# A three-part transformer kernel on one core: two gate products of the first mixture move from VectorE to GpSimd, and a copy moves one step later

## The chip, the cores and the metric

The kernel runs on one core of a Trainium2 chip. The metric is the device time of one execution in microseconds (us). The kernel before takes 2415.65 us, the median of 3 runs (2415.49 to 2415.98). In profiles the engines are PE (TensorE's matmuls), PEld (its weight loads), DVE (VectorE), ACT (ScalarE), POOL (GpSimd) and SP (SyncE, which issues all transfers).

## What is computed

4096 tokens of 256 features go through half a mixture of experts, an attention block with its own small feed-forward, and half the same mixture again, all in float32.

```python
def _L0_ffn_ref(x, gate_W, W1, b1, W2, b2, Ws1, bs1, Ws2, bs2, route_scale):
    B, S, D, E, H, K = (4, 512, 256, 8, 128, 2)
    scores = jax.nn.sigmoid(x @ gate_W) * route_scale
    topk_scores, topk_idx = jax.lax.top_k(scores, K)
    topk_w = topk_scores / topk_scores.sum(-1, keepdims=True)
    gate_full = jnp.einsum('bsk,bske->bse', topk_w, one_hot(topk_idx, E))
    h = jax.nn.gelu(jnp.einsum('bsd,edh->bseh', x, W1) + b1, approximate=False)
    y = jnp.einsum('bseh,ehd->bsed', h, W2) + b2
    shared = jax.nn.gelu(x @ Ws1 + bs1, approximate=False) @ Ws2 + bs2
    return jnp.einsum('bse,bsed->bsd', gate_full, y) + shared
...
x = x + 0.5 * _L0_ffn_ref(_layernorm(x), ...)
x = x + _L0_attn_ref(_layernorm(x), ...)
x = x + 0.5 * _L0_ffn_ref(_layernorm(x), ...)
```

## The kernel before

Four phases follow one another: the first mixture (names with `f_`, `tail` set), attention (`a_`), a small feed-forward (`m_`) and the second mixture (`g_`, the same function `ffn_phase` with `tail` not set). Instructions are written out by hand for each engine, in the order in which the engine runs them, and the engines meet at counted semaphores. An engine that waits holds up all that stands behind it on that engine.

A mixture handles the 4096 tokens in 8 blocks of 512. Blocks 0 and 1 are written out, blocks 2 to 5 are a loop over pairs, 6 and 7 are written out again. A block has nine steps: step 0 is the shared expert, steps 1 to 8 are the experts. For step e

- TensorE computes the hidden layer `hid` (`first_layer`, L938, 6 matmuls of 512 columns), and, two steps behind, the second layer of step e - 2 into `acc` (`second_layer`, L980, 12 matmuls of 256 columns). The second layer of step 7 runs in step 0 of the next block;
- ScalarE applies the gelu (L515), then, one step behind in `f_`, rounds the gated result to its high part (`hi`, L507);
- VectorE multiplies the gelu's result by the gate (`gating`, L737), and makes the low part (`lo`, L742), which in `f_` belongs to the step before and in `g_` from block 1 on mostly to the same step. The second layer waits for `lo`.

From block 2 on the gate of a token, laid out along the partitions, comes from SBUF (`gB`, filled by a transfer); in blocks 0 and 1 (`on_pe`) TensorE makes it in PSUM (`gbc`). So from block 2 on `gating` has two SBUF operands. `lo` has two SBUF operands always.

Between the steps VectorE does work for other blocks: the choice of the top two experts for block i + 1 (`choices` at step 3, `gates` at step 4, L701 to L720: a chain of small operations on 32 columns), the layer norm statistics and normalisation of block i + 2 (`x_stats` at step 6, `x_norm` at step 7, L652, which needs a power from GpSimd, L592), the copy of the stacked gates (`gate_stack`, L727, out of PSUM, at the step that `STEADY["stack"]` names), and in `f_` the statistics of the rows for attention (`z_stats` at step 2, `zz_stats` at step 5). GpSimd has only the powers and small products around them: L606 for the sigmoid, L589 to L602 for the norms. ScalarE's `z_norm` (step 4) and `zn_norm` (step 7), four operations each (L446), stand between its gelus. At step 8 of blocks 1 to 7 of `f_` TensorE transposes `zn` (L905 into `aux`). In block 1 that bank holds the stacked gates, so the transposes wait there for the copy of them:

```python
                if e == 8 and tail and not first:
                    if on_pe(i):
                        pe.wait_ge(s["gst"], i + 2)
                        pe.wait_ge(s["gf"], i)
```

In the other blocks TensorE waits for the copy only in step 0 of the next block, before it overwrites the bank. The code follows.

Of the kernel before, what the change touches and what calls it, by code (L numbers as in the profile page):

```python
# [23 lines left out]
ALU = mybir.AluOpType  # L24
# [8 lines left out]
E, HID = 8, 128  # L33
NE = E + 1
# [11 lines left out]
def stand_alone(eng, turns):  # L46


    eng.sem_inc(turns, 1)
# [75 lines left out]
def ffn_phase(nc, turns, tag, src, dst, w, tail):  # L125
# [17 lines left out]
    if tail:  # L143
# [21 lines left out]
        gated = m.sb("gated", [P, 3, BT], room=rooms.second)  # L165
# [9 lines left out]
        act_out = m.sb("act_out", [P, 3, BT], room=rooms.wide)  # L175
# [3 lines left out]
        gB = m.sb("gB", [P, E, BT], room=rooms.rows)  # L179
        gf = m.sb("gf", [P, BT], room=Rooms().loads)  # L180
# [14 lines left out]
    else:  # L195
# [9 lines left out]
        gB = m.sb("gB", [P, E, BT], room=rooms.wide)  # L205
        gf = m.sb("gf", [P, BT], room=rooms.wide)
# [7 lines left out]
        act_out = m.sb("act_out", [P, 3, BT], room=rooms.first)  # L214
        gated = m.sb("gated", [P, 3, BT], room=rooms.first)
# [30 lines left out]
    s = {n: m.sem(n) for n in names.split()}  # L246
# [7 lines left out]
    def shared(e):  # L254
        return e == 0

    def weights_of(e):
# [7 lines left out]
    PRODUCTS_AT = {2: 0, 3: 1, 5: 2}  # L265
    SUMS_AT = {3: 0, 4: 1, 6: 2}

    STEADY = dict(up_x=0, logits=1, neg=2, choices=3, gates=4, up_gates=6, gf=6, stack=6)
    FIRST = dict(stats=1, norm=2, up_x=3, logits=4, neg=5, choices=7, gates=7, up_gates=8, stack=8) if tail else \
        dict(stats=0, norm=1, up_x=2, logits=3, neg=4, choices=6, gates=7, up_gates=8, stack=8)  # L270

    def now(what, e, first):

        return (FIRST if first else STEADY).get(what) == e

    def has(i, ahead=0):

        return not isinstance(i, int) or 0 <= i + ahead < NB

    def on_pe(i):  # L280

        return isinstance(i, int) and i < 2

    def up_bank(i):

        return aux if on_pe(i) else gbc

    def over_blocks(eng, body):
        body(0, 0, True, False)
        body(1, 1, False, False)  # L290
        with eng.Fori(0, (NB - 4) // 2) as it:
            body(it * 2 + 2, 0, False, False)
            body(it * 2 + 3, 1, False, False)
        body(NB - 2, 0, False, False)
        body(NB - 1, 1, False, True)
# [274 lines left out]
    def on_gpsimd(pool):  # L570

        def first_fills():
            pool.memset(b2_in[:], 0.0)
            pool.memset(mhalf[:], -0.5)
            pool.memset(ebase[:], E_NUM)

        def pad():

            pool.memset(gpad[:], 0.0).then_inc(s["padded"], 1)
            pool.wait_ge(s["padded"], 1)  # L580
            pool.memset(gpad[:, :, 2 * E:LOW + E + 1:LOW - E], 1.0).then_inc(s["padded"], 1)
            pool.wait_ge(s["padded"], 2)

        def rstds(stats, ready, rstd, veps, powed, n, minus_mean=None):

            pool.wait_ge(ready, n)
            stand_alone(pool, turns)
            if minus_mean is not None:
                pool.tensor_scalar(minus_mean[:], stats[:, :, 0], -1.0, 0.0, ALU.mult, ALU.add)  # L589
            pool.tensor_scalar(rstd[:], stats[:, :, 1], EPS, None, ALU.add).then_inc(veps, 1)  # L590
            pool.wait_ge(veps, n)
            pool.tensor_tensor(rstd[:], rstd[:], mhalf[:], ALU.pow).then_inc(powed, 1)  # L592

        def x_rstd(i):
            rstds(mv, s["stats"], rs, s["veps"], s["rstd"], i + 1)

        def z_rstds(i, which):

            n = i * 2 + which + 1
            rstds(zmv, s["z_stats"], zrs, s["z_veps"], s["z_rs"], n, zshift)  # L600
            pool.wait_ge(s["z_rs"], n)
            pool.tensor_tensor(zshift[:], zshift[:], zrs[:], ALU.mult).then_inc(s["z_rstd"], 1)  # L602

        def expneg(i):
            pool.wait_ge(s["neg"], i + 1)
            pool.tensor_tensor(nl[:].rearrange("p t e -> p (t e)"), ebase[:],  # L606
                               nl[:].rearrange("p t e -> p (t e)"), ALU.pow).then_inc(s["expneg"], 1)

        def body(i, par, first, last):
            if first:  # L610
                x_rstd(1)
            if not last:
                expneg(i + 1)
            if tail and not first:
                z_rstds(i - 1, 0)
                z_rstds(i - 1, 1)
            if has(i, 2):
                x_rstd(i + 2)
        if tail:
            first_fills()  # L620
            pad()
            x_rstd(0)
        else:
            whole.mlp["gpsimd"](pool, dict(pad=pad, x_rstd=lambda: x_rstd(0), expneg=lambda: expneg(0)))
        over_blocks(pool, body)
        return dict(z_rstds=lambda which: z_rstds(NB - 1, which))

    def on_vector(dve):
# [100 lines left out]
        def gating(i, e):  # L729
            dve.wait_ge(s["gelu"], i * NE + e + 1)  # L730
            if on_pe(i):
                dve.wait_ge(s["gbc"], i * E + e)
                gate = gbc[:, (e - 1) % 2]
            else:
                dve.wait_ge(s["gates_in%d" % ((e - 1) // (E // 2))], (i - 1) * 16)
                gate = gB[:, e - 1]
            dve.tensor_tensor(gated[:, e % 3], gate, act_out[:, e % 3], ALU.mult).then_inc(s["gated"], 1)  # L737

# [88 lines left out]
        def body(i, par, first, last):  # L827
            for e in range(NE):
                if not last and now("neg", e, first):
                    neg_logits(i + 1, up_bank(i))  # L830
                if not shared(e):
                    gating(i, e)
                if e == 1 and not first:

                    result(i - 1)
                behind = not (tail or first) and e not in (0, 3, NE - 1)
                if tail or first:
                    if e > 0 and not (tail and first and e == 1):
                        lo(i, e - 1)
                    elif e == 0 and not first:  # L840
                        lo(i - 1, NE - 1)
                else:
                    if e == 0 and isinstance(i, int) and i == 1:
                        lo(0, NE - 1)
                    if not behind:
                        lo(i, e)
                if e == 0 and first:
                    gate_stack(0, 0, aux)
                if tail and first and e == 0:
                    qkv_bias(gbc[:, 1], 1, FIRST_BIAS)  # L850
                    w2_low(slice((NE - 1) * D, NE * D))
                if tail and first and e == 1:
                    w2_low(slice(0, (NE - 1) * D))
                if not last:
                    if now("stats", e, first):
                        x_stats(i + 1, 1 - par)
                    if now("norm", e, first):
                        x_norm(i + 1, 1 - par, False)
                    if now("up_x", e, first):
                        xt_lo(i + 1, 1 - par, up_bank(i))  # L860
                if tail and not first:
                    if e == 2:
                        z_stats(i - 1)
                    if e == 5:
                        zz_stats(i - 1)
                if not last:
                    if now("choices", e, first):
                        choices(i + 1)
                    if now("gates", e, first):
                        gates(i + 1)  # L870
                if has(i, 2):
                    if e == 6:
                        x_stats(i + 2, par)
                    if e == 7:
                        x_norm(i + 2, par, False)
                if not last and now("stack", e, first):
                    gate_stack(i + 1, 1 - par, up_bank(i))
                if tail and not first and e == 8:
                    for c in range(DC):
                        zt_lo(i - 1, c, aux[:, c])  # L880
                if tail and first and e == 2:
                    dve.wait_ge(s["qkv_in"], 64)
                    dve.tensor_scalar(ln[:, 0, :, 0], ln[:, 0, :, 0], QS, None, ALU.mult).then_inc(s["qs"], 1)
                    dve.wait_ge(s["qs"], 1)
                if tail and (first or last):
                    for k, c in QKV_AT.get((first, e), ()):
                        qkv_lo(k, c)
                if tail and last and e in SUMS_AT:
                    bias_sum(SUMS_AT[e])
                if behind:  # L890
                    lo(i, e)
# [1393 lines left out]
```

## Time and profile before

| | |
|---|---|
| median of 3 runs | 2415.65 us |
| the profiled execution | 2414.72 us, its span 2412.9 us |
| TensorE's granted clock | 0.999 of full speed |
| busy share of the span | PE 98%, PEld 86%, DVE 77%, ACT 70%, POOL 63% |
| first mixture | from 0 to about 276 us |
| second mixture | from about 2145 us to the end |
| period of a block, `f_` | about 31.4 us (block 4 to block 5) |
| period of a block, `g_` | about 29.5 us |

The span is from the first to the last instruction. A row of the timeline names the start in us, the duration, the engine, the line, the operation with its output and inputs, and how many like it follow one another. Idle time ahead of it, with what ended it, stands in brackets. In one engine's rows a start may lie up to 0.1 us before the end of the row above, since operations overlap a little.

### The profile page before, as it was taken

Reading aid. Unit: us, or ns where it says so; the run is one execution under the profiler, and the core shown is the slowest. Engines: PE = TensorE matmul, PEld = TensorE weight load, DVE = VectorE, ACT = ScalarE, POOL = GpSimd, SP = SyncE. Lnnn points to the kernel's source line nnn. Section 1 sums busy time; section 2 is a strip of 40 time slices with the busy share of each in tenths; the row PEclk is TensorE's granted clock in tenths of the full one; section 3 lists DMA queues with packets and bytes.
Section 4 is the critical chain, followed back from the end, with each engine's and each line's share of the span. In section 5 each row is a group of like instructions: output and inputs, shape, how many; then the busy total and the mean of one; then the engine's idle time right before and its main releaser. Section 6 shows DMA issues by size and latency. Waiting matters only on the chain.

```text
span 2412.9 us, 46345 instructions
## 1 busy us (share of the span) xinstructions
PE 2374.6 (98%) x14512; PEld 2068.2 (86%) x14512; DVE 1867.4 (77%) x3615; ACT 1684.6 (70%) x2932; POOL 1521.8 (63%) x1536
## 2 busy tenths in 40 slices
PE   8999999999999999999999999999999999999999
PEld 7888878888888888888888888888888889998898
DVE  7887687888878788887878878788887875466775
ACT  4555677877878787787878778787787865443444
POOL 1333368787777877778787777878777765542220
PEclk9999999999999999999999999999999999999999
DMA  4744631222212232221223312122221345431332
GB/s 181 264 165 156 211 114 45 96 80 78 96 44 87 61 96 75 64 96 44 87 62 97 102 36 96 44 87 84 82 96 44 110 165 166 137 116 58 130 125 95
DMA packets 131970, 245.67 MB, mean 102 GB/s; under 512 B 7290, under 2 KB 90132, under 8 KB 120052
## 3 DMA queue, kind: packets, MB, share of 16 engines
q1 hardware_dynamic: 131828, 244.15, 31.0%
q8 instruction: 44, 0.72, 0.1%
q14 instruction: 98, 0.80, 0.1%
HBM read 140.12 MB, written 53.67 MB: 80 GB/s over the span
## 4 chain that ended last, share of the span: by engine, by line
PE 83%; DVE 7%; issue 4%; POOL 3%; ACT 2%; DMA 2%; SPq 0%; DVEq 0%; POOLq 0%; ACTq 0%
PE a_ov L1727 20%; PE a_sc L1691 19%; PE a_tr L1703 19%; PE a_pj L1638 7%; PE a_pj L1645 4%; PE g_acc L980 3%; PE g_hid L938 3%; PE f_acc L980 2%; PE f_hid L938 2%; PE m_proj L2141 1%; POOL m_zin L1987 1%; PE m_hid L2210 1%; DMA f_xin<-in_x 1%; DVE f_hp L742 1%; DVE f_gated L737 1%
## 5 line engine op out<-in xcount | busy, mean ns | idle before, releaser
L1594 DVE TENSOR_REDUCE a_nmax<-a_sc 128x1 f32<-128x1024 f32 x512 | 626.8, 1224 | 252.1 <-PE a_sc L1691 248.3
L1437 ACT ACTIVATE a_pT<-a_tr 128x512 fp32r<-128x512 f32 x1024 | 559.6, 596 | 317.2 <-PE a_tr L1703 312.3
L1521 POOL TENSOR_SCALAR a_pr<-a_pr,a_rden 128x1024 f32<-128x1024 f32 x512 | 576.5, 1127 | 282.3 <-DVE a_rden L1599 212.1
L1605 DVE TENSOR_TENSOR a_pT<-a_tr,a_pT 128x512 fp32r<-128x512 f32 x1024 | 650.4, 677 | 17.1 <-ACT a_pT L1437 17.1
L1727 PE MATMUL a_ov<-a_pT,a_v_s 128*128 128x512 f32 x2032 | 594.1, 414 | 1.2 <-DVE f_zT L784 0.8
L1443 ACT ACTIVATE a_pr<-a_sc,a_nmax 128x1024 f32<-128x1024 f32 x512 | 573.7, 1121 | 20.2 <-DVE a_nmax L1594 17.9
L1691 PE MATMUL a_sc<-a_k_s,a_q_s 128*128 128x512 f32 x2048 | 556.6, 393 | 0.6 <-DMA a_k_s<-a_k_s 0.6
L1703 PEld LDWEIGHTS a_tr<-f_ident,a_pr 128*128 128x128 f32 x4096 | 476.0, 140 | 79.8 <-DVE a_pT L1605 7.3
L1703 PE MATMUL a_tr<-f_ident,a_pr 128*128 128x128 f32 x4096 | 537.1, 273 | 1.8 <-DVE a_pT L1605 1.7
L1691 PEld LDWEIGHTS a_sc<-a_k_s,a_q_s 128*128 128x128 f32 x2048 | 376.6, 188 | 76.7 <-DMA a_k_s<-a_k_s 0.8
L1727 PEld LDWEIGHTS a_ov<-a_pT,a_v_s 128*128 128x128 f32 x2032 | 343.8, 189 | 47.5 <-issue 4.8
L1638 PE MATMUL a_pj<-a_z_s,a_wqk_s 128*128 128x512 f32 x756 | 213.9, 392 | 1.5 <-ACT a_staged L1398 1.1
L1638 PEld LDWEIGHTS a_pj<-a_z_s,a_wqk_s 128*128 128x128 f32 x756 | 141.6, 188 | 33.7 <-ACT a_staged L1398 1.4
L980 PEld LDWEIGHTS f_acc<-f_w2p,f_hp 128*128 128x128 f32 x864 | 110.8, 190 | 19.5 <-DVE f_hp L742 14.6
L980 PE MATMUL f_acc<-f_w2p,f_hp 128*128 128x256 f32 x864 | 117.2, 285 | 7.4 <-DVE f_hp L742 7.1
L980 PEld LDWEIGHTS g_acc<-g_w2p,g_hp 128*128 128x128 f32 x864 | 111.9, 191 | 11.3 <-DVE g_hp L742 6.8
L980 PE MATMUL g_acc<-g_w2p,g_hp 128*128 128x256 f32 x864 | 115.7, 284 | 3.4 <-DVE g_hp L742 3.2
L1645 PEld LDWEIGHTS a_pj<-a_wv_s,a_z_s 128*128 128x128 f32 x756 | 105.8, 188 | 12.1 <-issue 0.7
L938 PE MATMUL f_hid<-f_xT,f_w1p 128*128 128x512 f32 x432 | 113.7, 398 | 0.0
L938 PE MATMUL g_hid<-g_xT,g_w1p 128*128 128x512 f32 x432 | 113.0, 397 | 0.0
L515 ACT ACTIVATE f_act_out<-f_hid,f_b 128x512 f32<-128x512 f32 x72 | 49.1, 684 | 91.0 <-PE f_hid L938 91.0
L1645 PE MATMUL a_pj<-a_wv_s,a_z_s 128*128 128x256 f32 x756 | 109.0, 280 | 0.3 <-ACT a_q_s L1405 0.3
(265 smaller groups left out, 3182.0 us busy)
## 6 DMA issues: line engine op xcount, KB each, us to landing
a_z_s<-zT SPq DMA_DIRECT2D x32, 1024.0 KB, 7.8
a_k_s<-a_k_s SPq DMA_DIRECT2D x62, 512.0 KB, 5.6
a_wqk_s<-w_split SPq DMA_DIRECT2D x64, 256.0 KB, 3.1
a_v_s<-a_v_b SPq DMA_DIRECT2D x16, 1024.0 KB, 4.6
att<-a_ao SPq DMA_DIRECT2D x32, 512.0 KB, 2.9
m_in<-att SPq DMA_DIRECT2D x16, 1024.0 KB, 5.9
f_gB<-f_gate_rows SPq DMA_DIRECT2D x12, 1024.0 KB, 4.9
g_gB<-g_gate_rows SPq DMA_DIRECT2D x12, 1024.0 KB, 4.7
```

What stands on the lines that cost most here:

```text
L938: o = pe.matmul(hid[:, (par + e) % 2], w1p[:, a, (c * NE + x) * HID:(c * NE + x + 1) * HID], xT[:, par, c, b], start=(n == 0), stop=(n == 5))
L980: o = pe.matmul(acc[:, t], hp[:, e % 3, a, t * P:(t + 1) * P], w2p[:, b, x * D:(x + 1) * D], start=False, stop=(e == NE - 1 and (a, b) == ...
L1437: act.activation(pT[:, (u // 4) % 2, 0, 4 * part:4 * part + 4, (u % 4) * P:(u % 4 + 1) * P], tr[:, part].rearrange("p (t q) -> p t q", t=4 ...
L1443: act.activation(pr[:, k % NP], sc[:, k % 2], ACT.Exp, bias=nmax[:, k % NP:k % NP + 1], accum_out=den[:, k % NP:k % NP + 1]).then_inc(s["e ...
L1521: pool.tensor_scalar(pr[:, k % NP], pr[:, k % NP], rden[:, k % NP:k % NP + 1], 1.0, ALU.mult, ALU.mult).then_inc(s["normed"], 1)
L1594: dve.tensor_reduce(nmax[:, k % NP:k % NP + 1], sc[:, k % 2], AX.X, ALU.max, negate=True).then_inc(s["negmax"], 1)
L1605: dve.tensor_tensor(to[:, 1], tr[:, part].rearrange("p (t q) -> p t q", t=4), to[:, 0].bitcast(F32), ALU.subtract).then_inc(s["tr_lo"], 1)
L1638: o = pe.matmul(bank[:], wqk_s[:, "QK".index(kind), h, a], z_s[:, h * 2 + b, part], start=(h == 0 and i == 0), stop=(h == 1 and i == 2), s ...
L1645: o = pe.matmul(bank[:, h * 2 * P:(h + 1) * 2 * P], z_s[:, c * 2 + a, part // 2, col:col + P], wv_s[:, c, b], start=(i == 0), stop=(i == 5))
L1691: o = pe.matmul(sc[:, k % 2, kb * BT:(kb + 1) * BT], q_s[:, slot, head, tile * P:(tile + 1) * P], k_s[:, slot, head, a, kb * BT:(kb + 1) * ...
L1703: o = pe.transpose(tr[:, part, j * P:(j + 1) * P], pr[:, (k - LAG) % NP, (4 * part + j) * P:(4 * part + j + 1) * P], ident[:])
L1727: o = pe.matmul(values_bank(v, last)[:], v_s[:, vslot, kt, 2 * vhead:2 * vhead + 2] .rearrange("p k f -> p (k f)"), pT[:, blk % 2, a, kt], ...
```

## The change

The products of the gates of experts 4 and 5 are issued by GpSimd in the first mixture's blocks 2 to 7, between its two groups of small operations for the norms. They write the same buffers and count on the same semaphore `gated`. VectorE leaves out these two, and its product for expert 6 waits until both are counted. In the steady blocks (1 to 6) of both mixtures the copy of the stacked gates moves from step 6 to step 7, where it stands after `x_norm`.

```diff
-    STEADY = dict(up_x=0, logits=1, neg=2, choices=3, gates=4, up_gates=6, gf=6, stack=6)
+    STEADY = dict(up_x=0, logits=1, neg=2, choices=3, gates=4, up_gates=6, gf=6, stack=7)
...
+    POOL_GATES = (4, 5)
...
+        def gating(i, e):
+
+            pool.wait_ge(s["gelu"], i * NE + e + 1)
+            pool.wait_ge(s["gated"], i * E + e - 1)
+            pool.wait_ge(s["gates_in%d" % ((e - 1) // (E // 2))], (i - 1) * 16)
+            stand_alone(pool, turns)
+            pool.tensor_tensor(gated[:, e % 3], gB[:, e - 1], act_out[:, e % 3], ALU.mult).then_inc(s["gated"], 1)
+
...
             if tail and not first:
                 z_rstds(i - 1, 0)
+                if not on_pe(i):
+                    for e in POOL_GATES:
+                        gating(i, e)
                 z_rstds(i - 1, 1)
...
                 dve.wait_ge(s["gates_in%d" % ((e - 1) // (E // 2))], (i - 1) * 16)
+                if tail and e == POOL_GATES[-1] + 1:
+
+                    dve.wait_ge(s["gated"], i * E + e - 1)
                 gate = gB[:, e - 1]
...
-                if not shared(e):
+                if not shared(e) and not (tail and not on_pe(i) and e in POOL_GATES):
                     gating(i, e)
```

How the rows move on the engines (line numbers of after are 13 to 16 higher on VectorE: L737 is L753 there, L742 is L758, L727 is L740). First VectorE, in a block of the first mixture's loop, from the choice at step 3 to the start of the chain of step 4. Before:

```order
L694 MAX_INDEX f_idx<-f_top,f_sg 128x8 x4
L678 REGISTER_ALU
L730 REGISTER_ALU
L737 TENSOR_TENSOR f_gated<-f_gB,f_act_out 128x512
L742 TENSOR_TENSOR f_hp<-f_gated,f_hp 128x512
L701 TENSOR_TENSOR f_ws<-f_top 128x4
```

After:

```order
L707 MAX_INDEX f_idx<-f_top,f_sg 128x8 x4
L691 REGISTER_ALU
L758 TENSOR_TENSOR f_hp<-f_gated,f_hp 128x512
L714 TENSOR_TENSOR f_ws<-f_top 128x4
L715 CAST f_idf<-f_idx 128x32
```

The product is gone, and the low part of step 3 comes right behind the choice. The same happens at step 5, between the end of the chain and the low part of step 4.

Then VectorE at steps 6 to 8 of the same block, from the statistics of block i + 2 to the low part of step 7. Before:

```order
L636 BN_AGGR f_mv<-f_st_89 128x2 x4
L727 CAST f_gst<-f_gbc 128x512
L730 REGISTER_ALU
L737 TENSOR_TENSOR f_gated<-f_gB,f_act_out 128x512
L742 TENSOR_TENSOR f_hp<-f_gated,f_hp 128x512
L650 REGISTER_ALU
L652 TENSOR_SCALAR f_xn<-f_xin,f_mv,f_rs 128x256 x4
L730 REGISTER_ALU
L737 TENSOR_TENSOR f_gated<-f_gB,f_act_out 128x512
L742 TENSOR_TENSOR f_hp<-f_gated,f_hp 128x512
```

After:

```order
L649 BN_AGGR f_mv<-f_st_89 128x2 x4
L743 REGISTER_ALU
L753 TENSOR_TENSOR f_gated<-f_gB,f_act_out 128x512
L758 TENSOR_TENSOR f_hp<-f_gated,f_hp 128x512
L663 REGISTER_ALU
L665 TENSOR_SCALAR f_xn<-f_xin,f_mv,f_rs 128x256 x4
L740 CAST f_gst<-f_gbc 128x512
L743 REGISTER_ALU
L753 TENSOR_TENSOR f_gated<-f_gB,f_act_out 128x512
L758 TENSOR_TENSOR f_hp<-f_gated,f_hp 128x512
```

The copy has passed the product of step 7, the low part of step 6 and the normalisation, and now stands ahead of the product of step 8 and the low part of step 7.

Last GpSimd in the same block, after the first group of norm operations. After (before, the row for L589, here L591, follows L602, here L604, with one register operation between):

```order
L604 TENSOR_TENSOR f_zshift<-f_zshift,f_zrs 128x4
L613 ISA
L614 ISA
L615 REGISTER_ALU
L617 TENSOR_TENSOR f_gated<-f_gB,f_act_out 128x512
L613 REGISTER_ALU
L614 REGISTER_ALU
L617 TENSOR_TENSOR f_gated<-f_gB,f_act_out 128x512
L588 REGISTER_ALU
L591 TENSOR_SCALAR f_zshift<-f_zmv 128x4
```

Two products with their waits now stand between the two groups.

## Rows read from the trace of the kernel before

**Rows 1.** The page, busy time and share of each engine

```profile
PE 2374.6 (98%) x14512; PEld 2068.2 (86%) x14512; DVE 1867.4 (77%) x3615; ACT 1684.6 (70%) x2932; POOL 1521.8 (63%) x1536
```

**Rows 2.** The timeline of PE, first mixture, blocks 4 and 2

```profile
168.54 1.70 PE L980 MATMUL f_acc<-f_w2p,f_hp 128*128 128x256 f32 x12
...
170.08 1.55 PE L938 MATMUL f_hid<-f_xT,f_w1p 128*128 128x512 f32 x6
171.97 1.70 PE L980 MATMUL f_acc<-f_w2p,f_hp 128*128 128x256 f32 x12 [0.35 <-DVE f_hp L742]
...
176.77 1.55 PE L938 MATMUL f_hid<-f_xT,f_w1p 128*128 128x512 f32 x6
178.63 1.70 PE L980 MATMUL f_acc<-f_w2p,f_hp 128*128 128x256 f32 x12 [0.31 <-DVE f_hp L742]
180.16 1.04 PE L905 MATMUL f_aux<-f_ident,f_zn 128*128 128x128 f32 x8
...
182.42 1.59 PE L980 MATMUL f_acc<-f_w2p,f_hp 128*128 128x256 f32 x12
...
115.54 1.70 PE L980 MATMUL f_acc<-f_w2p,f_hp 128*128 128x256 f32 x12 [0.64 <-DVE f_hp L742]
```

**Rows 3.** The timeline of DVE, first mixture, block 4

```profile
160.21 0.69 DVE L737 TENSOR_TENSOR f_gated<-f_gB,f_act_out 128x512 f32<-128x512 f32 x1 [1.51 <-ACT f_act_out L515]
...
167.80 0.68 DVE L742 TENSOR_TENSOR f_hp<-f_gated,f_hp 128x512 fp32r<-128x512 f32 x1
...
169.50 0.19 DVE L710 TENSOR_TENSOR f_ga<-f_ga,f_wt 128x32 f32<-128x32 f32 x1
...
171.23 0.69 DVE L742 TENSOR_TENSOR f_hp<-f_gated,f_hp 128x512 fp32r<-128x512 f32 x1
...
176.42 0.38 DVE L636 BATCH_NORM_AGGREGATE f_mv<-f_st 128x2 f32<-128x6 f32 x4 [0.15 <-DVE f_st L631]
176.71 0.66 DVE L727 CAST f_gst<-f_gbc 128x512 fp32r<-128x512 f32 x1
...
177.89 0.69 DVE L742 TENSOR_TENSOR f_hp<-f_gated,f_hp 128x512 fp32r<-128x512 f32 x1
179.00 1.38 DVE L652 TENSOR_SCALAR f_xn<-f_xin,f_mv,f_rs 128x256 f32<-128x256 f32 x4 [0.42 <-POOL f_rs L592]
...
180.90 0.69 DVE L742 TENSOR_TENSOR f_hp<-f_gated,f_hp 128x512 fp32r<-128x512 f32 x1
```

**Rows 4.** The timelines of POOL and ACT, first mixture, block 4

```profile
158.77 5.43 POOL L606 TENSOR_TENSOR f_nl<-f_ebase,f_nl 128x32 f32<-128x32 f32 x1 [11.34 <-DVE f_nl L668]
...
166.34 0.20 POOL L602 TENSOR_TENSOR f_zshift<-f_zshift,f_zrs 128x4 f32<-128x4 f32 x1
...
177.30 1.56 POOL L592 TENSOR_TENSOR f_rs<-f_rs,f_mhalf 128x4 f32<-128x4 f32 x1
...
168.69 0.67 ACT L515 ACTIVATE f_act_out<-f_hid,f_b 128x512 f32<-128x512 f32 x1
```

**Rows 5.** POOL's groups by line and shape: busy us, mean ns, idle before

```profile
L1500 POOL TENSOR_TENSOR a_k_s<-a_staged,a_k_s 64x512 fp32r<-64x512 f32 x62 | 80.5, 1298 | 3.6
...
L1544 POOL TENSOR_TENSOR a_ao<-a_ao,a_half 128x1024 f32<-128x1024 f32 x32 | 76.8, 2399 | 12.1 <-DVE a_half L1585 12.1
```

**Rows 6.** POOL's timeline at 2148 us; DVE line L652: min/median/max ns

```profile
2147.82 2.58 POOL L2052 TENSOR_TENSOR m_xin<-m_xin,m_h 128x1024 f32<-128x1024 f32 x1
...
L652 DVE TENSOR_SCALAR g_xn<-g_xin,g_mv,g_rs x2: 409/1459/2509, 2147.7 to 2148.0; 128x256 f32<-128x256 f32 x2
```

**Rows 7.** The timelines of DVE and PE, first mixture, block 1

```profile
81.28 0.38 DVE L636 BATCH_NORM_AGGREGATE f_mv<-f_st 128x2 f32<-128x6 f32 x4
...
83.35 1.39 DVE L652 TENSOR_SCALAR f_xn<-f_xin,f_mv,f_rs 128x256 f32<-128x256 f32 x4
...
85.03 1.04 PE L905 MATMUL f_aux<-f_ident,f_zn 128*128 128x128 f32 x8
```

**Rows 8.** The timelines of DVE and PE, second mixture, block 4

```profile
2320.46 0.68 DVE L742 TENSOR_TENSOR g_hp<-g_gated,g_hp 128x512 fp32r<-128x512 f32 x1
...
2321.58 1.60 PE L980 MATMUL g_acc<-g_w2p,g_hp 128*128 128x256 f32 x12
```

## Prediction

> **What bounds the kernel now.** The page comes first: TensorE is busy for 98% of the span [rows 1], so what counts is the 2% in which it waits, and what a change of order adds to that. Then the list of waits for the first mixture, and the timeline of a steady block. There the reader sees a second layer (L980) that starts late three times: those of steps 3, 4 and 6, at 168.54, 171.97 and 178.63 [rows 2]. Every time it is VectorE's low part that ends last: it starts at 167.80, 171.23 and 177.89 and takes 0.69, and TensorE starts 0.05 behind its end [rows 3]. A hidden layer is followed by the next group 1.39 later when nothing waits, so step 6's second layer, behind the hidden layer at 176.77, could start at 178.16: it is 0.47 late. The one of step 4, behind the hidden layer at 170.08, is 0.50 late, and that of step 3 about 0.3. A late group is also 0.1 longer, 1.70 against 1.59 [rows 2]: its first weights aren't loaded ahead. That makes about 1.6 us of 31.4 in a block. VectorE is the engine that sets these starts, and it has 0.61 less to do for each product that leaves (0.69 long, 0.08 of it over the next one) [rows 3].
>
> **What a product costs on GpSimd.** No row has 128x512. The nearest are 64x512 at 1.30 and 128x1024 at 2.40 [rows 5]; I take 1.3 (bounds 1.2 and 1.5). The product of expert 4 can start when the small operations end at 166.54, plus two waits and register work, some 0.25 (bounds 0.1 and 0.4): from 166.8 to 168.1. ScalarE needs it behind the gelu that starts at 168.69 [rows 4], so it is in time. The product of expert 5 starts behind that same gelu (0.67 long, and 0.2 for the wait), about 169.55, and ends at 170.85, before ScalarE wants it. VectorE's new wait at step 6 is over by then too. GpSimd's next work, the norm for zn, comes only after that. Taken alone the move would be free.
>
> **But the two engines get in each other's way.** At 2147.8 GpSimd adds 128x1024 in SBUF for 2.58 us, and VectorE's second normalising operation, issued at 2148.0, takes 2.51 instead of 0.41 [rows 6]: its work begins 0.25 before GpSimd's row ends. The power of block 4 shows the other direction: it takes 1.56 beside a product with two SBUF operands [rows 4]. So a GpSimd operation that streams from SBUF keeps out VectorE's operations with two SBUF operands. `lo` is one, and so are most of the small ones in the chain L701 to L720.
>
> - Step 3. `lo` could now start 0.61 before 167.80 [rows 3], but GpSimd streams until 168.1. It starts at 167.85. The 0.61 is lost, and step 3's second layer starts as before.
> - Step 4. The chain still starts behind `lo`, at 168.4. When GpSimd takes over at about 169.55 it stands at L710 (169.50) [rows 3]. It goes on at 170.6. What was left of it then took 1.13 us (it ended at 170.63, where step 4's product began, 0.6 before `lo`), so `lo` of step 4 starts at 171.73 instead of 171.23. TensorE starts 0.50 later than before: the relief of one product (0.6) against a hold of 1.1. Bounds of this delay: 0.2 (a hold of 0.8) and 1.0 (a hold of 1.3, and 0.3 brought along from step 3).
>
> **The copy one step later, blocks 3 to 5.** The rest of VectorE's work is 0.50 late too, but `lo` of step 6 no longer has the copy (176.71, 0.58 net) ahead of it: it starts at 177.89 + 0.50 - 0.58 = 177.81 and ends at 178.50. TensorE could start at 178.16 + 0.50 = 178.66, so it doesn't wait: +0.03 against before, and -0.07 without the slow start. The normalisation hangs on the statistics and the power, 2.58 behind 176.42 [rows 3], and so moves by 0.50. Behind it now stands the copy, then a product, then `lo` of step 7: 180.90 + 0.50 + 0.58 = 181.98, ending at 182.67. TensorE would come to this second layer at 182.42 - 0.07 = 182.35 [rows 2] and starts at 182.72: 0.30 late, and 0.1 more for the slow start. A block costs **0.4 more**, 1.2 for three.
>
> **Block 2.** Its step 6 waits longest, 0.64 in the row [rows 2], so it has more to win from the copy's leaving. I count 0 (bounds -0.3 and +0.4).
>
> **Blocks 6 and 7** have no normalisation ahead (6) or no copy either (7), so nothing is given back behind step 4: 0.5 from step 4 and about 0.1 from step 3. **0.6 each, 1.2** (bounds 0.2 and 1.0 each). In block 7 the long operations with two SBUF operands for the bias sums stand in for the chain.
>
> **Block 1, first mixture.** No product moves, but the copy does, and TensorE's transposes of zn wait for it there. They start at 85.03. The normalisation starts at 83.35, 2.07 behind the statistics [rows 7]. With `lo` drawn up beside the power this becomes 2.58, as in block 4: 83.86. Four operations, then the copy of 0.66, end at about 85.83, so the transposes start 0.85 later. **0.85** (lower bound 0.3: the normalisation stays at 83.35).
>
> **Second mixture.** No product moves. In blocks 2 to 5 `lo` of step 7 starts at 2320.46 and would end at 2321.75 with the copy ahead of it; TensorE is there at 2321.58 [rows 8]. It starts at 2321.80: 0.22 late and 0.1 slow. **1.3 for four blocks** (bounds 0 and 1.6). Block 1 has gate products on TensorE, so more slack, and block 6 has no normalisation: 0 for both, by their later second layers. Nothing there is repaid, since step 6 didn't wait.
>
> The sum: 1.2 + 0 + 1.2 + 0.85 + 1.3 = 4.55, on the profiled execution's 2414.72 it gives 2419.3. The median of the runs shown is 0.93 above that execution, so **2420.2 us**, +0.19%.
>
> On the hold there is a rule. The Trainium skill, page SBUF — State Buffer, section "SBUF: two separate sides", says of the port pair that both engines use that it is an exclusive lock: whoever starts first has it for the whole instruction, and the other fully blocks. It speaks against this change, and the rows agree on the direction. They differ in size. VectorE's work begins 0.25 before GpSimd's row ends [rows 6]; and during the power of 5.43 us at 158.77 [rows 4] a product with two SBUF operands runs in its usual 0.69 [rows 3]. By the rule to the letter both holds would be 0.25 longer; that would add about 0.4 to each of five or six blocks, and the sum would come to some 2422.
>
> **The rivals.**
>
> - *GpSimd hardly keeps VectorE out* (0.15). The power at 158.77 speaks for it: 5.43 us long, and the product at 160.21 isn't slowed. Against it is [rows 6], with an operation of the kind that is added. Then `lo` of steps 3 and 4 comes early, the waits of 0.31, 0.50 and 0.47 go with their slow starts, and only the copy's place costs something. Blocks 2 to 5 win about 1.4 each (1.6 less 0.2 for the copy ahead of step 7), 6 and 7 0.5 each: -6.6 + 0.85 + 1.3 = -4.45, 2411.2 us. This is the case on the other side. It decides from a hold under about 0.6, where what the products free pays for the copy.
> - *The hold is longer* (0.25). GpSimd's product starts or ends 0.3 later than I take it, and the delay of step 4 is 1.0. Then step 7 is late by as much. Blocks 3 to 5 cost 0.9 each, block 2 0.4, 6 and 7 1.1 each, and with 0.85 and 1.3 that is 7.45: 2423.1 us.
> - *The copy is free* (0.15). The power ends earlier when no copy stands beside it, or the lateness of step 7 is below what a trace shows. The second mixture costs 0, block 1 0.3: +2.7, 2418.4 us.
>
> **How the numbers follow.** The forecast gets 0.45, from 2418.5 to 2421.7 in itself. What a measurement of this kernel can tell from no change is about 0.2%, 4.8 us: 2420.5. My forecast lies just inside, so about half of it, 0.2, counts as slower and 0.25 as same. Slower: 0.2 + 0.25 less a little of the long hold = 0.43. Faster: nearly all of the first rival, 0.14. Same: 0.43. The range takes in the long hold and reaches to the first rival's near side: 2411.5 to 2424.
>
> **What would show it.** Right: GpSimd's products (two per block, 12 in all) of about 1.3 us; one of the small operations of the chain L701 to L720 (now L714 to L733) about 1 us long in blocks 2 to 6; step 4's second layer later by 0.5 behind its hidden layer, step 6's without a wait, step 7's with one, in both mixtures; the transposes of block 1 waiting for the copy. Wrong: a chain of unchanged length, which would make it faster, or products above 1.5 us.

## The result, and the profile after

The changed kernel takes 2420.9 us, the median of 15 runs (2419.49 to 2423.98), beside 2415.98 for the kernel before in the same session (15 runs, 2414.2 to 2419.76): a ratio of 1.0020, with a 95% interval from 1.0013 to 1.0028. It is slower by 4.9 us, which is little, but the interval doesn't reach 1. The execution whose trace is read here took 2422.76, with a span of 2420.9, so it is 1.9 above the median.

The busy times of the page, of the kernel after (it answers to [rows 1]):

```profile
PE 2379.0 (98%) x14512; PEld 2069.0 (85%) x14512; DVE 1871.2 (77%) x3603; ACT 1685.0 (70%) x2932; POOL 1536.2 (63%) x1548
```

Twelve instructions left VectorE (3615 to 3603) and came to GpSimd, yet VectorE's busy time did not fall, it rose by 3.8 us. Twelve products of 0.69 are gone. Something in its other rows grew by more than they were worth. The timelines say what.

The timeline of PE after, first mixture, block 4 (it answers to [rows 2]; the last row is step 4 of the next block):

```profile
170.15 1.69 PE L996 MATMUL f_acc<-f_w2p,f_hp 128*128 128x256 f32 x12 [0.23 <-DVE f_hp L758]
171.67 1.55 PE L954 MATMUL f_hid<-f_xT,f_w1p 128*128 128x512 f32 x6
174.09 1.70 PE L996 MATMUL f_acc<-f_w2p,f_hp 128*128 128x256 f32 x12 [0.87 <-DVE f_hp L758]
...
178.89 1.55 PE L954 MATMUL f_hid<-f_xT,f_w1p 128*128 128x512 f32 x6
180.28 1.67 PE L996 MATMUL f_acc<-f_w2p,f_hp 128*128 128x256 f32 x12
181.78 1.04 PE L921 MATMUL f_aux<-f_ident,f_zn 128*128 128x128 f32 x8
182.57 1.63 PE L954 MATMUL f_hid<-f_xT,f_w1p 128*128 128x512 f32 x6
184.46 1.70 PE L996 MATMUL f_acc<-f_w2p,f_hp 128*128 128x256 f32 x12 [0.25 <-DVE f_hp L758]
...
206.11 1.69 PE L996 MATMUL f_acc<-f_w2p,f_hp 128*128 128x256 f32 x12 [0.85 <-DVE f_hp L758]
```

Step 4's second layer comes 2.42 behind its hidden layer at 171.67, so it is 1.03 late where it was 0.50. Step 6's, at 180.28, comes 1.39 behind 178.89 and doesn't wait. Step 7's, at 184.46, now does: 1.89 behind its hidden layer, where [rows 2] and the hidden layer at 180.96 of before gave 1.46. (A step 7 that doesn't wait stands 1.46 behind its hidden layer, since that one starts slowly behind the transposes; steps 3, 4 and 6 stand 1.39 behind.) From step 4 to step 4 a block takes 206.11 - 174.09 = 32.02 us; before it was 31.44.

The timeline of DVE after, the same block (it answers to [rows 3]):

```profile
168.57 1.53 DVE L758 TENSOR_TENSOR f_hp<-f_gated,f_hp 128x512 fp32r<-128x512 f32 x1
...
171.22 1.30 DVE L724 TENSOR_TENSOR f_gb__101<-f_gb__101,f_wt 128x32 f32<-128x32 f32 x1
...
173.35 0.69 DVE L758 TENSOR_TENSOR f_hp<-f_gated,f_hp 128x512 fp32r<-128x512 f32 x1
...
178.63 0.38 DVE L649 BATCH_NORM_AGGREGATE f_mv<-f_st 128x2 f32<-128x6 f32 x4 [0.15 <-DVE f_st L644]
...
181.22 1.38 DVE L665 TENSOR_SCALAR f_xn<-f_xin,f_mv,f_rs 128x256 f32<-128x256 f32 x4 [1.03 <-POOL f_rs L594]
182.52 0.68 DVE L740 CAST f_gst<-f_gbc 128x512 fp32r<-128x512 f32 x1
...
183.72 0.68 DVE L758 TENSOR_TENSOR f_hp<-f_gated,f_hp 128x512 fp32r<-128x512 f32 x1
```

And POOL's, which has the two products (it answers to [rows 4]):

```profile
167.88 0.20 POOL L604 TENSOR_TENSOR f_zshift<-f_zshift,f_zrs 128x4 f32<-128x4 f32 x1
168.25 1.30 POOL L617 TENSOR_TENSOR f_gated<-f_gB,f_act_out 128x512 f32<-128x512 f32 x1 [0.17 <-issue]
171.17 1.29 POOL L617 TENSOR_TENSOR f_gated<-f_gB,f_act_out 128x512 f32<-128x512 f32 x1 [1.62 <-ACT f_act_out L517]
```

The two are read side by side. `lo` of step 3 is issued at 168.57, while the product of expert 4 runs, and takes 1.53 instead of 0.69. The 128x32 operation at 171.22 takes 1.30 instead of 0.19, while the product of expert 5 runs. Each is held until just before GpSimd's row ends. That is VectorE's busy time that did not fall: it waits inside its rows.

The timeline of PE after in block 1, where no product moved (it answers to [rows 7]); the transposes wait for the copy, as their bracket says:

```profile
86.14 1.09 PE L921 MATMUL f_aux<-f_ident,f_zn 128*128 128x128 f32 x8 [0.72 <-DVE f_gst L740]
```

### The profile page after: what moved, and what is told of

Read it like the earlier page. It is cut to its first block, busy times and chain, and to the rows that moved or that the text cites. A ratio compares the mean times of both kernels' runs of the same rounds, so it can differ in the third digit from the quotient of the medians.

```text
span 2420.9 us, 46378 instructions
## 1 busy us (share of the span) xinstructions
PE 2379.0 (98%) x14512; PEld 2069.0 (85%) x14512; DVE 1871.2 (77%) x3603; ACT 1685.0 (70%) x2932; POOL 1536.2 (63%) x1548
## 4 chain that ended last, share of the span: by engine, by line
PE 81%; DVE 9%; issue 4%; POOL 3%; ACT 2%; DMA 1%; SPq 0%; DVEq 0%; POOLq 0%; ACTq 0%
PE a_ov L1743 20%; PE a_sc L1707 19%; PE a_tr L1719 19%; PE a_pj L1654 7%; PE a_pj L1661 4%; PE g_acc L996 2%; PE g_hid L954 2%; PE f_acc L996 2%; PE f_hid L954 2%; PE m_proj L2157 1%; DVE f_hp L758 1%; POOL m_zin L2003 1%; PE m_hid L2226 1%; DVE f_gated L753 1%; DVE f_zst L644 0%
```

## The experiments

Times are medians, each beside the kernel before on the same chip in the same session (2415.32, 2415.28 and 2415.17 in the three sessions). The kernel before itself had medians from 2415.17 to 2415.98, and a ratio's interval is 4 to 5 us wide, so what is small is read from the traces: how late a second layer starts, and the period of a block, from block 4 to block 5.

**The two halves apart.** First the products alone, the copy where it was:

```diff
-    STEADY = dict(up_x=0, logits=1, neg=2, choices=3, gates=4, up_gates=6, gf=6, stack=7)
+    STEADY = dict(up_x=0, logits=1, neg=2, choices=3, gates=4, up_gates=6, gf=6, stack=6)
```

> The two products on GpSimd as in the change, the copy of the gate stack at step 6 as before. If the hold of the shared port is what costs (my theory), blocks 2 to 7 of the first mixture are each about 0.6 us longer than before (step 3 by 0.1, step 4 by 0.5, and the wait of step 6 stays at 0.47), block 1 and the second mixture are as before: +3.6 us, 2419.6. If the copy's new place were what costs (rival), this kernel would be as before, 2416, or faster, 2411.

Measured: 2417.49 us, ratio 1.0012 [1.0003, 1.0021]. The timeline of PE, block 5:

```profile
204.79 1.69 PE L996 MATMUL f_acc<-f_w2p,f_hp 128*128 128x256 f32 x12 [0.85 <-DVE f_hp L758]
...
209.57 1.55 PE L954 MATMUL f_hid<-f_xT,f_w1p 128*128 128x512 f32 x6
211.54 0.74 PE L996 MATMUL f_acc<-f_w2p,f_hp 128*128 128x256 f32 x4 [0.41 <-DVE f_hp L758]
```

Step 4 is as late as in the changed kernel (1.0), and step 6 is 1.97 - 1.39 = 0.58 late, for the copy is still ahead of its `lo`. The period is 32.10, against 31.44 before. The last transposes of zn in the first mixture come 2.7 later than before, 3.0 if the 0.36 is counted by which block 1 began earlier; the second mixture is as before. So the products cost about 3 us in the trace, and 2.2 between the medians (the interval goes from 0.7 to 5.1).

Then the copy alone, in the kernel before:

```diff
-    STEADY = dict(up_x=0, logits=1, neg=2, choices=3, gates=4, up_gates=6, gf=6, stack=6)
+    STEADY = dict(up_x=0, logits=1, neg=2, choices=3, gates=4, up_gates=6, gf=6, stack=7)
```

> All products on VectorE as before, only the copy of the gate stack at step 7. My theory: in the first mixture block 1 is 0.8 us longer (the transposes wait for the copy), blocks 2 to 5 a little shorter (the wait of step 6 goes, one of about 0.3 at step 7 comes: -0.15 each); in the second mixture blocks 2 to 5 are 0.33 longer each. Sum +0.8 - 0.6 + 1.3 = +1.5, 2417.5. If the copy is free (rival), 2415 or below and no new wait in the second mixture.

Measured: 2417.51 us, ratio 1.0008 [0.9999, 1.0017]. The timeline of PE, blocks 1 and 4:

```profile
85.62 1.09 PE L905 MATMUL f_aux<-f_ident,f_zn 128*128 128x128 f32 x8 [0.70 <-DVE f_gst L727]
...
178.64 1.60 PE L980 MATMUL f_acc<-f_w2p,f_hp 128*128 128x256 f32 x12
...
182.71 1.46 PE L980 MATMUL f_acc<-f_w2p,f_hp 128*128 128x256 f32 x10 [0.21 <-DVE f_hp L742]
```

In block 4 the wait of step 6 is gone and step 7's has come: 0.39 late (1.85 behind its hidden layer, against 1.46). They cancel, the period is 31.36. What the copy costs stands elsewhere: some 0.8 in block 1 (85.62 against 85.03 in [rows 7], and 0.17 more because this execution reached the block 0.17 earlier), and in the second mixture a step 7 that is 0.21 late in each of blocks 2 to 5, with a period of 29.76 against 29.47. Between the medians the two halves add up, 2.2 + 2.2 = 4.4 us beside 4.9 for the whole change, but each has an interval of 2 us to either side, and the copy's reaches below zero. The traces say it better: 3.0 for the products and 0.5 + 1.2 in the two mixtures for the copy make 4.7, and the changed kernel's two mixtures are 4.8 longer.

**Is it how long GpSimd streams?** The changed kernel, with GpSimd's products cut to 128 of their 512 columns. This leaves three quarters of the products of experts 4 and 5 out of the computation.

```diff
-            pool.tensor_tensor(gated[:, e % 3], gB[:, e - 1], act_out[:, e % 3], ALU.mult).then_inc(s["gated"], 1)
+            pool.tensor_tensor(gated[:, e % 3, 0:128], gB[:, e - 1, 0:128], act_out[:, e % 3, 0:128], ALU.mult).then_inc(s["gated"], 1)
```

> The change with GpSimd's products cut to 128 of 512 columns (three quarters of two gate products are left out); all waits, semaphores and the order are those of the change. If the time that GpSimd streams is what holds VectorE (my theory), step 3's low part loses at most 0.3 and the operation held in the chain of step 4 falls from 1.30 to about 0.4 us; blocks 2 to 5 become about 1.5 us shorter than in the change, and the kernel comes to some 2413. If the new waits or their latency cost (rival), it stays at 2420 to 2421.

Measured: 2413.1 us, ratio 0.9990 [0.9981, 0.9999]. Of the timelines of POOL and of DVE, block 4, the rows on both sides of the hold:

```profile
169.21 0.47 POOL L617 TENSOR_TENSOR f_gated<-f_gB,f_act_out 128x128 f32<-128x128 f32 x1 [2.45 <-ACT f_act_out L517]
...
169.27 0.45 DVE L732 COPY f_gpad<-f_ga 128x32 f32<-128x32 f32 x1
```

The hold shrinks with the product: 0.28 (0.45 instead of 0.17). Steps 3 and 4 are no longer late from block 3 on, and the period is 30.37, which is 1.1 under before. So with a hold of about 0.3 most of what the rival promised, in which GpSimd hardly keeps VectorE out, does come (1.4 a block, 2411.2 us). The new waits and the order are those of the change, so it isn't they that cost. One thing more: what was held is a COPY with a single SBUF operand, which the theory had not listed. And block 2 did not win its share. Its step 6 starts 1.65 late:

```profile
112.74 1.41 DVE L644 BATCH_NORM_STATS2 f_st<-f_xin 128x6 f32<-128x256 f32 x4 [1.58 <-DMA f_xin<-in_x]
```

The statistics wait there for the load of x. In the kernel before the same row waits 0.24 for it, in the changed one not at all, and in the run below with one operand 1.14: what is won ahead of a transfer can be lost to it again.

**Must GpSimd read two operands?** The changed kernel, with the products on GpSimd replaced by the activation times a constant. This leaves the gates of experts 4 and 5 out.

```diff
-            pool.tensor_tensor(gated[:, e % 3], gB[:, e - 1], act_out[:, e % 3], ALU.mult).then_inc(s["gated"], 1)
+            pool.tensor_scalar(gated[:, e % 3], act_out[:, e % 3], 0.5, 0.0, ALU.mult, ALU.add).then_inc(s["gated"], 1)
```

> The changed kernel with the two gate products on GpSimd replaced by the activation times a constant (so the gates of experts 4 and 5 are left out of the result): the GpSimd instruction reads one SBUF operand and not two. Theory: it is the two SBUF operands that GpSimd streams which keep VectorE out; with one, the instruction of the gate chain is back from 1.30 to about 0.19 us, steps 3 and 4 are no longer late, the block period falls from 32.0 to about 30.4 us, and the time is near that of the quarter products, 2413 us. Rival: any GpSimd instruction on SBUF of that length keeps VectorE out; the chain's instruction stays over 1 us, step 4 stays 1.0 us late, and the time stays near 2420 us.

Measured: 2414.05 us, ratio 0.9994 [0.9984, 1.0003]. The timelines of POOL and of DVE, block 4:

```profile
166.29 0.63 POOL L617 TENSOR_SCALAR f_gated<-f_act_out 128x512 f32<-128x512 f32 x1 [0.19 <-issue]
169.19 0.63 POOL L617 TENSOR_SCALAR f_gated<-f_act_out 128x512 f32<-128x512 f32 x1 [2.27 <-ACT f_act_out L517]
...
166.58 0.88 DVE L758 TENSOR_TENSOR f_hp<-f_gated,f_hp 128x512 fp32r<-128x512 f32 x1
...
169.24 0.61 DVE L730 COPY f_gpad<-f_ghi 128x32 f32<-128x32 f32 x1
```

The time came out near the theory's number, but its condition falls. GpSimd reads one operand here and still holds VectorE: `lo` takes 0.88, a copy of 128x32 takes 0.61 in place of 0.18. What made the kernel faster is that the instruction is shorter, 0.63 for 128x512 in place of 1.30. The rival (any GpSimd instruction on SBUF of that length holds) is right on the mechanism and wrong on the size, since it took the instruction to be as long. Step 4 is 0.17 late and the period 30.71: between the quarter products (0.47 us long) and the full ones, as their lengths are.

**Which of the two products?** Each alone, with the copy at step 6 (`stack=6` as above):

```diff
-    POOL_GATES = (4, 5)
+    POOL_GATES = (4,)
```

> Expert 4's product alone on GpSimd, the copy at step 6 as before. Theory: the GpSimd product takes the place of 1.3 us of VectorE work (product and subtraction) ahead of the gate chain, the subtraction of step 3 ends as before, and the chain itself isn't touched, so step 4 stays about 0.5 us late, the block period stays 31.4 us and the time that of before (within 0.5 us). Rival (each product costs by its own, half of the loss each): period 31.75, time 1.3 us over before.

Measured: 2415.31 us, ratio 1.0001 [0.9992, 1.0010]; step 4 is 0.52 late, and the period 31.48. The timelines of POOL and DVE, block 4:

```profile
165.83 1.30 POOL L617 TENSOR_TENSOR f_gated<-f_gB,f_act_out 128x512 f32<-128x512 f32 x1 [0.17 <-issue]
...
166.14 1.53 DVE L758 TENSOR_TENSOR f_hp<-f_gated,f_hp 128x512 fp32r<-128x512 f32 x1
```

And with `POOL_GATES = (5,)`:

> Expert 5's product alone on GpSimd, the copy at step 6 as before. Theory: this is the product that lies over the gate chain; one 128x32 instruction of it is held for about 1.1 us, the product's 0.6 us on VectorE is saved, so step 4 is about 1.0 us late, the block period is 32.1 us and the time that of the two products together, 2.2 to 3 us over before. Rival (each product costs by its own): period 31.75, time 1.3 us over before.

Measured: 2418.46 us, ratio 1.0015 [1.0006, 1.0025]; step 4 is 0.93 late, and the period 31.94. The timelines of POOL and DVE in this run:

```profile
170.19 1.30 POOL L617 TENSOR_TENSOR f_gated<-f_gB,f_act_out 128x512 f32<-128x512 f32 x1 [3.15 <-ACT f_act_out L517]
...
170.32 1.21 DVE L725 TENSOR_TENSOR f_ga<-f_ga,f_gb__101 128x32 f32<-128x32 f32 x1
```

The cost is all in expert 5's product, the one that runs while VectorE is in the gate chain. Expert 4's costs nothing and gains nothing: 0.6 us leave VectorE, and `lo`, issued 0.8 earlier, is held 0.84. (That expert 5's product alone shows 3.2 between the medians, and both products 2.2, is within the intervals; in the two traces the last transposes of zn come at 273.21 and 273.25.) That the two halves of a loss are equal, the rival of both runs, is refuted.

**A product where VectorE has other work.** In steps 5 and 6 VectorE computes statistics (1.4 us each time, one SBUF operand read and little written). So expert 6's product goes to GpSimd instead, with the copy at step 6:

```diff
-    POOL_GATES = (4, 5)
+    POOL_GATES = (6,)
```

> One product on GpSimd, that of expert 6, and the copy at step 6 as before. In the trace of before GpSimd would stream it from about 172.6 to 173.9 of block 4, while VectorE does its batch norm statistics, which have one SBUF operand. If only operations with two SBUF operands are held (my theory), no operation of VectorE is held for long, the low part of step 6 comes 0.6 earlier, the wait of step 6 (0.47 and 0.1 of slow start) goes in blocks 3 to 5: -1.7 us, 2414.3. If any GpSimd stream holds any VectorE operation (rival), the statistics take 1.3 longer, step 5 and 6 are late, and it is 2418 or more.

Measured: 2415.11 us, ratio 0.9999 [0.9990, 1.0008]. The timelines of POOL and DVE, block 4:

```profile
171.70 1.29 POOL L617 TENSOR_TENSOR f_gated<-f_gB,f_act_out 128x512 f32<-128x512 f32 x1 [6.14 <-ACT f_act_out L517]
...
170.84 1.39 DVE L644 BATCH_NORM_STATS2 f_zst<-f_zz 128x6 f32<-128x256 f32 x4
...
172.69 0.85 DVE L758 TENSOR_TENSOR f_hp<-f_gated,f_hp 128x512 fp32r<-128x512 f32 x1
```

The four statistics that end at 172.23 keep their 1.39 although for the last 0.53 the product runs beside them, from 171.70; only `lo` is held, by 0.16. The period falls to 31.03, 0.4 less than before, and the last transposes of zn come 1.1 earlier (269.12 against 270.58, less the 0.34 by which block 1 began earlier). The expected 1.7 was too much: step 6 no longer waits, but its second layer still has the slow start (1.70). Between the medians only 0.2 is seen. In the last block the transposes of zn had to wait for ScalarE:

```profile
269.12 1.06 PE L921 MATMUL f_aux<-f_ident,f_zn 128*128 128x128 f32 x8 [0.66 <-ACT f_zn L448]
```

So the next run left that block's product on VectorE:

```diff
-                if not on_pe(i):
+                if not on_pe(i) and not last:
                     for e in POOL_GATES:
...
-                if not shared(e) and not (tail and not on_pe(i) and e in POOL_GATES):
+                if not shared(e) and not (tail and not on_pe(i) and not last and e in POOL_GATES):
```

> Expert 6's product on GpSimd, copy at step 6, in blocks 2 to 6 of the first mixture; the last block as before. With expert 6's product in the last block too the time was 0.2 us under before (2415.1), and the transposes at the last block's end waited 0.66 us for ScalarE. Theory: in the last block nothing else of VectorE's is worth hiding and the GpSimd product only delays the chain behind it; about 0.6 us less than with the product in all blocks, 2414.5 us, 0.8 us under before. Rival: that wait is made up for behind it, 2415.1 us as with the product in all blocks.

Measured: 2414.57 us, ratio 0.9994 [0.9985, 1.0003]. The wait of 0.66 is gone, and from the transposes of block 6 to those of block 7 it is 28.42, against 28.79 with the product in all blocks and 28.41 in the kernel before: the product cost 0.4 in the last block, where 0.6 was expected. Yet the last transposes come at 269.18, no earlier than 269.12. The two kernels are the same up to the last block, but in this execution the statistics of block 2 waited 0.69 for the load of x and not 0.45, which made that block 0.3 longer, and it had reached block 1 0.2 later. Half a microsecond between two medians is no more than the kernel before shows against itself; the time of this run decides nothing, its trace bears the reason out.

**Using the room.** Expert 6's product away from VectorE leaves room in steps 5 to 7. Into it went the last four instructions of the gate chain, which step 4 waits for, and the copy, in blocks 2 to 6 of the first mixture:

```diff
             dve.tensor_copy(ghi[:], ga[:]).then_inc(s["gate"], 1)
+        def gate_pad(i):
             dve.wait_ge(s["gate"], (i + 1) * GC)
...
                 if tail and not first:
+                    if e == 5 and not last:
+                        gate_pad(i + 1)
...
                         gates(i + 1)
+                        if not tail or first:
+                            gate_pad(i + 1)
...
-                if not last and now("stack", e, first):
+                if not last and (e == 7 if tail and not on_pe(i) else now("stack", e, first)):
```

> Expert 6's product on GpSimd in blocks 2 to 6, the last four instructions of the gate chain (the writes of the padded gates, 0.36 us on VectorE) moved from step 4 to step 5, and the copy at step 7 in blocks 2 to 6 of the first mixture alone. Theory: with expert 6's product off VectorE, steps 5 to 7 have room for 0.36 us of the chain and for the copy; step 4's second layer is then 0.15 us late and not 0.5, step 6 isn't late, step 7 about 0.15 late; the block period falls from 31.03 to about 30.7 us, and the time to 2413 us, 2.3 us under before. Rival: VectorE works without a pause from step 3 to step 7, so that what is moved only turns up as a later step 6 or 7; period 31.0, 2414.6 us.

Measured: 2413.69 us, ratio 0.9995 [0.9986, 1.0004], the lowest median of a kernel that leaves nothing out; the interval still takes in 1. The timeline of PE, block 4:

```profile
170.80 1.70 PE L1003 MATMUL f_acc<-f_w2p,f_hp 128*128 128x256 f32 x12
...
176.98 1.66 PE L1003 MATMUL f_acc<-f_w2p,f_hp 128*128 128x256 f32 x12
...
179.27 1.63 PE L961 MATMUL f_hid<-f_xT,f_w1p 128*128 128x512 f32 x6
181.14 1.10 PE L1003 MATMUL f_acc<-f_w2p,f_hp 128*128 128x256 f32 x7 [0.25 <-DVE f_hp L759]
```

Step 4 comes 1.49 behind its hidden layer at 169.31, only 0.1 late, and step 6 doesn't wait. But step 7 starts 0.41 late (1.87 against 1.46), where 0.15 was expected, and the period is 31.01, as without the two moves. The rival is right in the steady blocks: the wait has gone to step 7. What the trace shows as won, 0.6 to 0.7 at the last transposes of the first mixture (268.48, against 269.12 and 269.18 without the moves), lies nearly all in block 2. But there the two kernels without the moves, which are the same up to that point, differ by 0.4 themselves (116.50 and 116.94, beside 116.21), so how much the moves are worth stays open. The same two moves in the kernel before:

> The kernel before with the same two moves (the writes of the padded gates at step 5, the copy at step 7 in blocks 2 to 6 of the first mixture) and all products on VectorE. Theory: without a product taken off VectorE the moves only shift the wait: step 4 0.15 us late, step 7 about 0.8 late in place of step 6's 0.47; period 31.4 us, time that of before within 0.5 us. Rival (the chain is what is late, wherever the products run): period 31.1, about 1.8 us under before.

Measured: 2414.25 us, ratio 0.9998 [0.9989, 1.0008]; step 4 is 0.12 late, step 7 0.42, and the period 31.30. Between the theory (31.4) and its rival (31.1), and nearer to the theory. With the copy at step 7 that step is 0.4 late whatever was taken off VectorE ahead of it (0.39 to 0.43 in block 4 of the four kernels that have it there for the steady blocks): its `lo` stands behind the copy, the copy behind the normalisation, and that hangs on GpSimd's power behind the statistics.

## Why the prediction was right, point by point

The forecast was 2420.2, the time 2420.9. That the two medians are only 0.7 apart is in part luck, since the interval is nearly 4 us wide; what bears the forecast out is its terms, on the traces:

- **The product's length.** 1.3 was taken from [rows 5]; the twelve rows show 1.28 to 1.30, but for one of 2.33 in block 7, which ran beside VectorE's bias sum of 1.28. Right.
- **Step 3.** `lo` was held by 0.84 (1.53 against 0.69) and the second layer came 0.08 later than before: what the product freed was lost. Right in blocks 4 and 5; in blocks 2 and 3, where it was 0.55 late before, it came 0.17 earlier. The run with expert 4's product alone shows the hold by itself.
- **Step 4.** Predicted 0.50 later, measured 0.53; a hold of 1.11 in the chain against 1.1 predicted. Right, and shown by the run with expert 5's product alone and by the two with shorter instructions.
- **Step 6.** Its wait of 0.47 went. Right, but its slow start stayed: the row is 1.67 long, where 1.59 was taken.
- **Step 7.** The forecast had TensorE there at 182.35 and starting at 182.72, 0.37 late (its 0.30 counts from the start of before, 182.42). Measured it is 0.43, 1.89 against 1.46. VectorE brought 0.62 along to the end of the statistics where I carried 0.50: from the hidden layer of step 4 to the row behind the statistics it was 6.34 before [rows 2, 3] and is 6.96 (171.67 to 178.63).
- **Blocks 3 to 5.** This is the term that was too small. From step 4 to step 4 it is 0.58 and not 0.4: step 3 adds 0.05 to 0.08 where nothing was taken, step 7 0.06, and the slow start of step 6 that wasn't won back 0.07. Block 3 costs 0.35, since its step 3 gained. Together 1.5, against 1.2 predicted.
- **Block 2:** 0 predicted, 0.02 measured. **Blocks 6 and 7:** 0.6 each, measured 0.58 and 0.63. **Block 1:** 0.85 predicted, 0.83 measured (the transposes start 0.78 later and run slowly), from the normalisation now 2.49 behind the statistics and the copy in its way. **Second mixture:** 1.3 predicted; the trace shows step 7 late by 0.22 to 0.24 in blocks 2 to 5, which with the slow starts is 1.4, and the whole stretch 1.2 longer. The first mixture's terms sum to 3.25, and the trace shows 3.6 once the 0.33 is taken off by which its execution started later.

The spans of the two traces differ by 8.0, though, not by 4.8. The rest, some 3, lies in attention and in the hand-over behind it, where no instruction moved, and at the start. The traced executions account for it: the one after is 1.9 above its median, the one before (2414.72) 1.3 below that of its session.

Two of the reasons given were less right than the sum. First, the prediction said that GpSimd holds only VectorE's operations with two SBUF operands, and the expectation of the one-operand run added that GpSimd too must read two. One operand on GpSimd is enough, and a plain copy from SBUF to SBUF is held as well as an operation with two SBUF operands (the statistics, with one, are not). The row that the prediction rested on was already of that kind: the normalisation of [rows 6] streams one tensor, its other two operands being one value per partition. That made no difference to the sum, since nearly all of the chain is of one kind or the other. Of the Trainium skill, the page SBUF — State Buffer, section "SBUF: two separate sides", counts on VectorE's side both the operations with two SBUF inputs, against a GpSimd operation that reads SBUF, and those in a two-port performance mode; it asks for no second operand on GpSimd. The traces agree with it there (the copy took 0.61 beside the one-operand instruction of 0.63); whether the copy ran in such a mode no trace shows.

Second, the end of the hold. From [rows 6] I had VectorE's work begin 0.25 before GpSimd's row ends. In the rows above, taking each usual length off a held row's end: `lo` of step 3 began at 170.10 - 0.69 = 169.41, and GpSimd's row ends at 169.55; the 128x32 operation at 172.52 - 0.19 = 172.33 against 172.46; with one operand 169.85 - 0.18 = 169.67 against 169.82. That is 0.13 to 0.15. What the Trainium skill says in that section, that the one that starts first "gets the pair for the whole instruction", is so nearly right for GpSimd's products. It doesn't fit the power of 5.43 us [rows 4], beside which products and `lo` of VectorE keep their 0.69, in every one of these traces.

## What to carry to other kernels

Work moved from VectorE to GpSimd leaves VectorE only if VectorE meanwhile runs what GpSimd doesn't hold. So before moving a product, lay its expected row over the other engine's timeline. Beside a subtraction from SBUF it gains nothing, and over a chain of small dependent operations it costs nearly its whole length, more than it saved. Statistics it doesn't hold, nor operations that take one operand out of PSUM. In the attention of the kernel before, two such operations run in their usual 1.27 beside a product of two SBUF operands:

```profile
329.38 1.29 POOL L1500 TENSOR_TENSOR a_q_s<-a_staged,a_q_s 64x512 fp32r<-64x512 f32 x1
...
329.44 1.27 DVE L1605 TENSOR_TENSOR a_pT<-a_tr,a_pT 128x512 fp32r<-128x512 f32 x2
```

Where one engine sets the pace through several steps in a row, moving an operation a step later moves the wait with it, unless some stretch between is idle; and a table of steps that several stages share charges the move in all of them, also in those that had nothing to win.

## What the runs showed of the hardware

- GpSimd takes 1.28 to 1.30 us for a product of 128x512 in f32 with two SBUF operands, 0.46 to 0.47 for 128x128, and 0.63 for 128x512 times a constant. VectorE takes 0.69 for the product.
- A held VectorE row shows as a long row, not as idle time: 1.30 for an operation of 0.19. The list of waits says nothing of it. Busy time that doesn't fall when instructions leave is the sign.
- It works in the other direction too. In block 7 the product on GpSimd met VectorE's bias sum of 128x1024 and took 2.33; with one operand it took 1.54 there in place of 0.63. The rows of the changed kernel:

```profile
261.90 1.28 DVE L789 SCALAR_TENSOR_TENSOR f_qkv_in<-f_qkv_in,f_ln 128x1024 f32<-128x1024 f32 x1
...
262.00 2.33 POOL L617 TENSOR_TENSOR f_gated<-f_gB,f_act_out 128x512 f32<-128x512 f32 x1
```

- Whether GpSimd's 5.43 us power lets VectorE through because it reads so few elements (128x32) was not tried, and stays open.
